# A fused attention and mixture-of-experts layer: the constant under the roots on GpSimd, the scatter in five steps, and new step lists

## The reference

```python
# 1: flow attention, 16 heads of 16, then a feed-forward block
q, k, v = sigmoid(x@Wq+bq), sigmoid(x@Wk+bk), x@Wv+bv
sink_in = n / sum((q+eps) * (cumsum(k)+eps));  src_out = n / sum((k+eps) * (cumsum(q)+eps))
cons_sink = sum((q+eps) * (cumsum(k*src_out)+eps)) / n
cons_src  = exp(clip(sum((k+eps) * (cumsum(q*sink_in)+eps)) / n, -1, 1))
a = q*sink_in/n @ cumsum(k (x) v*cons_src/cumsum(cons_src)*n) * sigmoid(cons_sink)
h = layernorm(x + a@Wo+bo)*g1+b1;  h = layernorm(h + gelu(h@W1+c1)@W2+c2)*g2+b2
x = layernorm(x + h)
# 2: eight experts of width 1024, each token goes to the one with the largest logit
e = argmax(x@router.T);  x = layernorm(x + square(relu(x@fc[e]))@proj[e].T)
```

## Time and profile before

| | |
|---|---|
| median of 3 runs | 828.53 us |
| lowest, highest | 828.28, 829.38 us |
| span of the profiled execution | 827.1 us |
| PE busy | 781.0 us (94%) |
| VectorE (DVE) busy | 579.8 us (70%) |
| GpSimd (POOL) busy | 337.6 us (41%) |
| ScalarE (ACT) busy | 309.9 us (37%) |
| chain that ended last | PE 88%, DVE 5%, issue 2%, ACT 2%, POOL 1% |

### The profile page before, as it was taken

How to read it: one execution, slowest core, us unless ns; L and a number is a source line. 1 busy time by engine, 2 the same in 40 slices (tenths; PEclk the granted TensorE clock), 3 DMA queues, 4 the chain that set the end, 5 groups by cost and what they waited for, 6 DMA issues and landing times.

```text
span 827.1 us, 18739 instructions
## 1 busy us (share of the span) xinstructions
PE 781.0 (94%) x6828; PEld 599.1 (72%) x6828; DVE 579.8 (70%) x1339; ACT 309.9 (37%) x571; POOL 337.6 (41%) x433
## 2 busy tenths in 40 slices
PE   7988899999999999999999989989999999999994
PEld 3466677677687687677777777778998787777762
DVE  7988878898988889889898884783654433433432
ACT  2333323523523633533543433342123444334442
POOL 8211513423642741750661663463324333234434
PEclk9999999999999999999999999999999999999998
DMA  7999995100100100100000032683769897878850
GB/s 252 279 330 329 325 323 174 52 1 2 52 28 1 53 27 2 52 27 2 27 27 2 27 112 107 204 282 100 252 209 380 341 337 294 329 293 299 296 203 13
DMA packets 75194, 133.22 MB, mean 161 GB/s; under 512 B 5726, under 2 KB 54112, under 8 KB 75105
## 3 DMA queue, kind: packets, MB, share of 16 engines
q1 hardware_dynamic: 71936, 123.57, 44.4%
q0 software_dynamic: 3168, 8.46, 2.8%
HBM read 89.35 MB, written 42.93 MB: 160 GB/s over the span
## 4 chain that ended last, share of the span: by engine, by line
PE 88%; DVE 5%; issue 2%; ACT 2%; POOL 1%; DMA 0%; POOLq 0%; ACTq 0%; SPq 0%; DVEq 0%
PE bank L950 11%; PE bank L985 11%; PE bank L837 7%; PE bank L849 7%; PE bank L869 6%; PE bank L880 6%; PE bank L649 6%; PE bank L799 5%; PE bank L815 4%; PE bank L765 4%; PE bank L997 4%; PE bank L965 4%; PE bank L658 2%; PE bank L687 2%; PE bank L679 2%
## 5 line engine op out<-in xcount | busy, mean ns | idle before, releaser
L1300 POOL TENSOR_TENSOR rstd<-vare,minus_half 128x1 f32<-128x1 f32 x96 | 59.2, 618 | 255.0 <-DVE vare L1575 254.5
L950 PE MATMUL bank<-xsT,fc 128*128 128x128 f32 x800 | 95.8, 279 | 0.7 <-issue 0.7
L950 PEld LDWEIGHTS bank<-xsT,fc 128*128 128x128 f32 x800 | 93.4, 195 | 3.7 <-issue 3.4
L1566 DVE TENSOR_TENSOR sm<-bank,upto 128x512 f32<-128x512 f32 x128 | 79.4, 682 | 19.1 <-PE bank L765 19.1
L985 PE MATMUL bank<-pj,act 128*128 x336 | 76.1, 380 | 0.5 <-issue 0.5
L1161 ACT ACTIVATE relu<-bank 128x512 f32<-128x512 f32 x68 | 40.1, 595 | 86.9 <-PE bank L950 59.0
L837 PE MATMUL bank<-n1T,w1s 128*128 128x256 f32 x256 | 67.5, 386 | 2.9 <-ACT hT L1110 2.4
L869 PE MATMUL bank<-n1T,w1s 128*128 128x256 f32 x256 | 67.4, 386 | 1.3 <-ACT hT L1127 0.8
L985 PEld LDWEIGHTS bank<-pj,act 128*128 128x128 f32 x336 | 62.3, 190 | 8.2 <-issue 0.7
L1355 POOL TENSOR_TENSOR mrstd<-mvare,minus_half 128x1 f32<-128x1 f32 x34 | 19.3, 566 | 118.8 <-DVE mvare L1784 118.8
L880 PE MATMUL bank<-w2s,hT 128*128 128x256 f32 x256 | 66.3, 387 | 0.3 <-ACT hT L1127 0.3
(11 more groups left out here) (267 smaller groups left out, 1644.4 us busy)
## 6 DMA issues: line engine op xcount, KB each, us to landing
routed_rows<-empty SPq DMA_DIRECT2D x64, 520.0 KB, 8.3
fc<-in_fc SPq DMA_DIRECT2D x31, 1024.0 KB, 6.7
up_unit<-in_fc SPq DMA_DIRECT2D x24, 1024.0 KB, 8.3
pj<-in_pj SPq DMA_DIRECT2D x8, 1024.0 KB, 12.3
xrow<-in_fc SPq DMA_DIRECT2D x6, 1024.0 KB, 6.9
...
```

The costliest lines, as they stand in the source:

```text
L950: last = nc.tensor.matmul(h_bank[n][:, chunk(f)], fc[:, at, k, chunk(4 * n + f)], xsT[:, k, :], start=(k == 0), stop=(k == KT - 1))
L1300: nc.gpsimd.tensor_tensor(rstd[:, n, c], vare[:, n, c], minus_half[:], ALU.pow)\
L1566: nc.vector.tensor_tensor(sm[:, n], BANK4[n][:].rearrange("p (h t) -> p h t", h=4), upto[:].unsqueeze(1).broadcast_to([P, 4, P]), ALU.mult ...
```

## The change

Three things change in code, and all the step lists.

1. The addition of 1e-5 moves from VectorE to GpSimd, where it stands directly ahead of the power, as `(x + 1e-5) * 1.0`. `c_sum2`'s next VectorE instruction now waits for bn_aggr itself.
2. `d_count` on GpSimd is cut into five: `d_ids` (the ids) and four steps `d_count` 0 to 3 with one indirect DMA each.
3. `turn_k` (p_kt) gets waits, since it now stands ahead of `p_pairs`.

```diff
@@ turn_k, PE
                 if c == 0:
+                    ev["kp"].wait(pe, g, KT)
+                    if g == 0:
+                        pe.wait_ge(masks_done, ALL_MASKS)
+                        ev["v"].wait(pe, 1, 4)
@@ rsqrt, GpSimd
+                ev[f"ba{n + 1}"].wait(pool, g, c + 1)
+                nc.gpsimd.tensor_scalar(vare[:, n, c], mv[:, n, c, 1:2], EPS_LN, 1.0, ALU.add, ALU.mult)\
+                    .then_inc(S[f"ve{n + 1}"], 1)
                 ev[f"ve{n + 1}"].wait(pool, g, c + 1)
@@ scatter, GpSimd
-            def scatter(g, half, _):
+            def next_ids(g, half, _):
                 wait_scattered(pool, g, half)
                 ...
                 nc.gpsimd.tensor_scalar(mine, mine, L, None, ALU.add).then_inc(ids_next, 1)
+            def scatter(g, half, c):
+                if c == 0:
+                    pool.wait_ge(ids_next, g + 1)
+                    ... (the rows, the emptied tiles, the slots)
-                for c in range(NC):
-                    nc.gpsimd.indirect_dma_start(...)
+                nc.gpsimd.indirect_dma_start(...)
@@ store (routed tiles), GpSimd
+                M["aggr"].wait(pool, j, 1)
+                nc.gpsimd.tensor_scalar(mvare[:, j % 3], mmv[:, j % 3, 1:2], EPS_LN, 1.0, ALU.add, ALU.mult)\
+                    .then_inc(M["vare"].sem, 1)
@@ stats, finish, VectorE
-                nc.vector.tensor_scalar(vare[:, n, c], mv[:, n, c, 1:2], EPS_LN, None, ALU.add)...
-                nc.vector.tensor_scalar(mvare[:, s], mmv[:, s, 1:2], EPS_LN, None, ALU.add)...
```

The lists, in the parts that the prediction speaks of (each line is one engine's order; `x n` is the step's index):

```diff
@@ DVE_FIRST (group 0 unless told)
-a_proj 0..3, a_prod, a_proj 4, 5, a_dots1, t_head, a_share1, a_scan2 0, 1, t_xb, a_proj(1) 4, a_dots2,
+a_proj 0, t_head, a_proj 1..3, a_prod, a_proj 4, 5, a_dots1, t_xb, a_share1, a_scan2 0, 1, a_proj(1) 4, t_half1 0, a_dots2,
@@ PE_ORDER
-p_share2, d_count, a_proj 0, b_turn 0, a_proj 1 2 3, b_turn 1, a_proj 4, b_up 0, a_proj 5, p_kt 0, b_down 0, b_up 1,
-p_pairs 0, b_up 2, b_down 1, b_down 2, b_up 3, p_mix 0, a_dots1, p_out 0, b_down 3, b_up 4, c_route 0, p_pairs 1, p_kt 1,
-b_up 5, b_down 4, p_mix 1, p_out 1, b_up 6, a_share1, b_down 5, b_up 7, b_down 6, c_route 1, h_turn 0, p_pairs 2, h_turn 1,
-b_down 7, h_up 0, p_kt 2, h_up 1, h_down 0, ..., p_mix 2, a_dots2, p_out 2, ..., p_mix 3, a_comp, p_out 3, h_up 6, ...
+p_share2, d_count, b_turn 0, a_proj 0 1, b_turn 1, a_proj 2 3 4, b_up 0, a_proj 5, p_kt 0, b_up 1, b_down 0, b_up 2,
+p_pairs 0, b_down 1, b_up 3, b_down 2, p_mix 0, a_dots1, b_up 4, p_out 0, b_down 3, p_pairs 1, c_route 0, b_down 4, p_kt 1,
+b_up 5, p_mix 1, b_down 5, p_out 1, b_up 6, a_share1, b_up 7, c_route 1, b_down 6, h_turn 0, b_down 7, h_turn 1, p_kt 2,
+h_up 0, p_pairs 2, h_up 1, h_down 0, ..., p_mix 2, a_dots2, p_out 2, ..., p_mix 3, a_comp, h_up 6, c_route 3, p_out 3, ...
@@ DVE_ORDER
-..., c_sum2 0, 1, a_proj 0..5, a_prod, p_mask 0..3, c_sum3 0, 1, p_state 0, a_dots1, p_sums 0, p_mask 4..7, b_half, c_sum2 2,
-p_state 1, p_sums 1, a_share1, a_scan2 0, 1, p_mask 8..11, c_sum3 2, c_sum2 3, p_state 2, a_dots2, p_sums 2, ...
+..., c_sum2 0, a_proj 0..5, a_prod, p_mask 0..3, c_sum2 1, c_sum3 0, p_state 0, a_dots1, p_sums 0, c_sum3 1, p_mask 4..7,
+c_sum2 2, p_state 1, c_sum3 2, p_sums 1, c_sum2 3, a_share1, b_half, a_scan2 0, p_mask 8..11, a_scan2 1, c_sum3 3, a_dots2, ...
@@ ACT_ORDER
-p_share2, b_turn 0, a_proj 0 1 2, b_turn 1, a_proj 3, b_up 0, ...
+b_turn 0, a_proj 0 1, b_turn 1, a_proj 2 3, p_share2, b_up 0, ...
@@ POOL_ORDER
-p_xb, p_split, d_count, c_sum2 0, 1, c_sum3 0, 1, p_mix 0, 1, c_sum2 2, c_sum3 2, p_norm 0, 1, c_sum2 3, b_turn, p_mix 2, ...
+d_ids, p_xb, p_split, d_count 0, c_sum2 0, d_count 1, c_sum2 1, d_count 2, c_sum3 0, p_mix 0, c_sum2 2, c_sum3 1, p_norm 0,
+p_mix 1, b_turn, d_count 3, c_sum3 2, c_sum2 3, p_norm 1, p_mix 2, c_sum3 3, ...
@@ the ..._LAST lists
 on GpSimd d_count 5, 6 and 7 are cut up among c_sum2, c_sum3 and m_store; the last, d_count(7) 3, stands behind m_store 4
 on VectorE d_units and d_placed of group 7 stand one tile (m_finish) later
```

More of the change, by code:

```diff
@@ L124 @@
[L124 to L127, removed]
+    ("p_out", 0, 1), ("a_share1", 1, 0), ("p_kt", 0, 2), ("h_turn", 0, 0), ("h_turn", 0, 1), ("p_pairs", 0, 2),
@@ L128 @@
+    ("h_up", 0, 0), ("h_down", 0, 0), ("h_up", 0, 1), ("p_mix", 0, 2), ("h_up", 0, 2), ("h_down", 0, 1),
+    ("h_up", 0, 3), ("p_out", 0, 2), ("a_dots2", 1, 0), ("h_up", 0, 4), ("h_down", 0, 2), ("p_kt", 0, 3),
+    ("p_pairs", 0, 3), ("h_up", 0, 5), ("h_down", 0, 3), ("p_mix", 0, 3), ("a_comp", 1, 0), ("p_out", 0, 3),
+    ("h_down", 0, 4), ("h_up", 0, 6), ("h_down", 0, 5), ("h_up", 0, 7), ("h_down", 0, 6), ("h_down", 0, 7),
 ]
 PE_ORDER = [
-    ("p_share2", 0), ("d_count", 0), ("a_proj", 0), ("b_turn", 0), ("a_proj", 1), ("a_proj", 2), ("a_proj", 3),
@@ L132 @@
[L132 to L140, removed]
+    ("p_share2", 0), ("d_count", 0), ("b_turn", 0), ("a_proj", 0), ("a_proj", 1), ("b_turn", 1), ("a_proj", 2),
+    ("a_proj", 3), ("a_proj", 4), ("b_up", 0), ("a_proj", 5), ("p_kt", 0), ("b_up", 1), ("b_down", 0), ("b_up", 2),
@@ new lines @@
+    ("p_pairs", 0), ("b_down", 1), ("b_up", 3), ("b_down", 2), ("p_mix", 0), ("a_dots1", 0), ("b_up", 4),
+    ("p_out", 0), ("b_down", 3), ("p_pairs", 1), ("c_route", 0), ("b_down", 4), ("p_kt", 1), ("b_up", 5),
+    ("p_mix", 1), ("b_down", 5), ("p_out", 1), ("b_up", 6), ("a_share1", 0), ("b_up", 7), ("c_route", 1),
+    ("b_down", 6), ("h_turn", 0), ("b_down", 7), ("h_turn", 1), ("p_kt", 2), ("h_up", 0), ("p_pairs", 2),
+    ("h_up", 1), ("h_down", 0), ("h_up", 2), ("h_down", 1), ("h_up", 3), ("h_down", 2), ("h_up", 4), ("p_mix", 2),
@@ L141 @@
+    ("a_dots2", 0), ("p_out", 2), ("c_route", 2), ("h_down", 3), ("p_pairs", 3), ("p_kt", 3), ("h_down", 4),
+    ("h_up", 5), ("p_mix", 3), ("a_comp", 0), ("h_up", 6), ("c_route", 3), ("p_out", 3), ("c_logit", 0),
+    ("h_down", 5), ("h_up", 7), ("c_back", 0), ("h_down", 6), ("h_down", 7),
 ]
 PE_LAST = [
-    ("b_turn", 7, 0), ("m_turn", 0, 0), ("b_turn", 7, 1), ("d_count", 5, 0), ("b_up", 7, 0), ("b_up", 7, 1),
-    ("b_down", 7, 0), ("b_up", 7, 2), ("b_down", 7, 1), ("b_up", 7, 3), ("b_down", 7, 2), ("c_route", 6, 0),
@@ L199 @@
+    ("h_turn", 0, 1), ("h_up", 0, 0), ("h_up", 0, 1), ("h_up", 0, 2), ("p_mix", 0, 2), ("h_up", 0, 3),
+    ("p_pairs", 0, 3), ("h_up", 0, 4), ("p_norm", 0, 2), ("a_dots2", 1, 0), ("p_mix", 0, 3), ("h_up", 0, 5),
+    ("h_up", 0, 6), ("p_norm", 0, 3), ("h_up", 0, 7),
 ]
 ACT_ORDER = [
[L202 to L203 removed]
@@ L204 @@
[L204 to L208 removed]
+    ("b_turn", 0), ("a_proj", 0), ("a_proj", 1), ("b_turn", 1), ("a_proj", 2), ("a_proj", 3), ("p_share2", 0),
```

146 lines of the change are left out of this document (73 added, 73 removed), and 5 rows, old and new, of tables (DVE_LAST, POOL_LAST).

## The result

The changed kernel took 821.41 us (median of four runs, 817.9 to 823.8) beside 828.95 of the kernel before (828.3 to 829.9): ratio 0.988, 95% interval 0.985 to 0.992. In a later session it took 818.8 beside 830.9 (0.986, 0.982 to 0.989). The nine runs together have a median of 820.5. Its profiled execution has a span of 819.8 us, 7.3 less than before. The forecast was 822.6, faster.

A forecast was written before the change was run, and what follows sets the result against it. PE was nearly always busy from 91 to 817 us, so only its idle time, and VectorE's chain in the first stage, could be won. Terms +2.3-0.5-3.5-1.8-2.7+0.3 = -5.9 gave 821.2, plus 1.4: 822.6 us, range 817.0 to 830.5.

The forecast's parts named there:

- 1, the start: First stage: VectorE's `t_xb`, moved ahead of `a_share1`, waits for the router's weights and delays the chain; +2.3 us, bounds 0 to 3.5.
- 2, the period of group 2: Period of group 2: PE's 2.2 us wait for the value tile at `p_pairs` shrinks; -0.5 us, bounds 0 to -1.0.
- the slower rival: Second scans: VectorE becomes late beside GpSimd's long operations, through the shared ports; 831.6 us, chance 0.16.
- 3, the full periods: Five steady periods: moved steps cover PE's small waits, 0.7 us gained in each; -3.5 us, bounds 0 and -5.3.
- 4, the last period: Last period: `b_turn` 0 moves ahead on ScalarE, so waits on `n1T` and `xat` shrink; -1.8 us, bounds 0 and -2.8.
- 5, the change-over: Change-over to the experts: scatters issued singly between roots remove PE's waits for routed row and expert tile; -2.7 us.
- the cut of the scatter adds no DMA: nothing: GpSimd's scatter: issuing the four transfers as separate steps was claimed to cost nothing.
- 6, the constant: Addition under the roots, moved to GpSimd: each root 0.3 us later, paid only by the very last tile; +0.3 us.
- the lists leave 0.5 us or more for both: Steady periods: ScalarE's n1 and xrow, behind a root 0.3 us later, were claimed to have 0.5 us or more cover.
- (a): Rival: VectorE becomes late at the second scans, delaying a_dots2 by 1.5 us in six periods; 831.6 us, chance 0.16.
- (b): Rival: gaps only move in steady periods, and last period and change-over gain half; -0.1 us, 828.4 us, chance 0.12.
- (c): Rival: the start costs nothing and all gaps close; -10.5 us, 818.0 us, chance 0.15.

## Why the prediction came out right, step by step

**1, the start: the mechanism right; the excess is mostly the clock of one run (+2.3, measured +6.2 in the profile shown).** The product's delay was 3.6 us, inside the 2.9 to 4.0 forecast. At 43.85 PE's first `p_share2` was 4.2 us late (39.64 before), but in two other profiles of the same steps it stood at 40.63 and 41.75; the profile shown had a granted clock of 0.79 at 34 to 42 us, all the others 1.00 up to 46. The stage itself ended at 97.56, 95.92 (the run again) and 94.17 (the kernel with the scatter block, whose first stage is instruction for instruction the changed one), and with the constants on VectorE at 97.13. With the old first lists the ends are 91.39, 91.50, 91.57, 93.06, 94.83 and 94.99. They compare only at like clocks. Where the mean granted clock up to 92 us was 0.96, the old lists ended at 91.5 and 91.6 and the changed ones at 94.2; where it was 0.93, at 94.8 and 95.0 against 95.9 and 97.6. So the step is worth 1 to 2.7 us, and the 2.3 lies in it. The stall with `t_xb` has 1.1 of that by either pair: 94.17 against 93.08 with the step put back, and 95.93 against 94.83 in the old lists. What the term lacked was the clock: the earlier trace rows gave 0.98 there, and I took a stage's clock as fixed. Of the medians none shows the step; runs spread too far.

**2, the period of group 2 (-0.5, measured -3.0): mis-sized.** That the later start made it short, which I tried with the old first lists, isn't so: it is short with either start. Three things came that the term didn't have (that these are the whole of it is read off the rows, not shown by a run). The wait on `n1T` at the head of this period, the largest of the three in the earlier trace rows, stood at 95.08 and goes with the same move of `b_turn` on ScalarE that I priced only for the last period. The timeline of the kernel before, and of the changed one:

```profile
95.08 0.41 PE L860 MATMUL bank<-ident,n 128*128 128x128 f32 x2 [2.19 <-ACT n1T L1121]
...
104.01 1.15 PE L765 MATMUL bank<-qm,kT 32*128 32x256 f32 x16 [2.24 <-DVE vpad L1479]
...
136.28 2.27 PE L799 MATMUL bank<-sm,vpad 128*32 128x128 f32 x29
```

```profile
99.63 0.41 PE L868 MATMUL bank<-ident,n 128*128 128x128 f32 x2 [0.57 <-ACT n1T L1129]
...
101.42 3.54 PE L662 MATMUL bank<-wqkv,xT 128*128 128x256 f32 x8 [1.38 <-DVE kT L1576]
```

The wait on `n1T` fell from 2.19 to 0.57. The value tile's 2.24 went too, and 0.9 on the query product, against a new 1.38 on the key product. And `p_mix` 2 took 2.27 us for 29 matmuls, at full clock, where the changed kernel has 1.12 for 32: a stretched group of matmuls that shows as busy and hides a wait. The masks that it waits for stood behind VectorE's second scans. The timelines of VectorE and GpSimd, before and changed:

```profile
124.98 7.66 DVE L1450 TENSOR_TENSOR_SCAN cc<-ones_t,cc 128x512 f32<-128x512 f32 x4
128.29 3.26 POOL L1294 TENSOR_TENSOR x<-x,be2s 128x1024 f32<-128x1024 f32 x1
```

```profile
128.91 2.37 POOL L1302 TENSOR_TENSOR x<-x,be2s 128x1024 f32<-128x1024 f32 x1
131.38 3.27 DVE L1467 TENSOR_TENSOR_SCAN cc<-ones_t,cc 128x512 f32<-128x512 f32 x2
```

The rule of the Trainium skill that I had weighed for the slower rival (page "SBUF — State Buffer", section "SBUF: two separate sides") pays out here on the gain's side: the last of the four scans took 3.31 us beside the wide addition, 1.2 where nothing stands beside one, and in the changed kernel the addition is over before the scans begin and the masks come after two of them. The trace doesn't bear out "in full" for every operation: beside the masked queries (1.6 to 2.2 us each, at 100.04 to 103.77) the changed kernel's scans took 1.21 and 1.65, though the profile's spans on GpSimd are rough. And the pair of the earlier trace rows is not where the 3 us come from: with the old first lists it took 4.63 beside the same addition, and the period was as short, 58.2. Nor is 3.0 a firm figure: the old period took 61.0, 61.1, 61.1, 62.7 and 62.7 us in five kernels with the same steps in it, the new one 58.0 to 58.2 in nine.

**3, the full periods (-3.5, measured -3.1): right.** 0.86, 0.70, 0.39, 0.71 and 0.40. The waits at `p_out` 1 and 3 are gone. The margin was nearly used up: 0.15 us of slack at `a_dots2`, not 0.7. With the constants back on VectorE the next thin place shows, the masks at `p_mix` 1, with 0.5 us.

**4, the last period (-1.8, measured -1.1): the size a little off.** The prediction took 2 of the 4.1 us on `n1T` for this period; it was 1.53, since the 2.2 in the earlier trace rows is group 2's. It fell to 0.56, and of the 1.4 us on `xat` 1.0 went; a new one of 0.5 us stands at `p_kt` (on `acc`), which now comes sooner.

**5, the change-over (-2.7, measured -6.4): right in sign, wrong in its reason.** I priced the removal of PE's waits at 555 with the cut as the cause. The cut alone costs 4.1 us in the old lists and, taken away, 7.2 in the new. What it does depends on what PE, VectorE and ScalarE have around it: the new order has `c_choose`, the squares and the expert tiles where their waits are covered. The old change-over also held more than the idle time that I priced: of the 6.4 us, 4.0 are idle time of PE over the whole part (6.1 to 2.0 us) and 2.3 are busy time, with a granted clock of 0.98 in the old one (0.96 in its first 46 us) and 1.00 in the new. The step that failed is "the cut of the scatter adds no DMA: nothing". It has a due time, the reuse of `xrow` two groups on.

**6, the constant (+0.3, measured +0.1 at the end): wrong as a whole.** The last tile's output multiply waits 0.97 us for its root, 0.69 before; but VectorE's own addition ahead of it is gone, and the tail as a whole is 0.1 us longer (192.3 in all ten profiles with the constant on GpSimd, 192.2 in the four without). The term had 0.3 us for the addition and 0.2 for the wait behind it; in this tile they are 0.19 and 0.09. In the steady periods it is free, as said. But "the lists leave 0.5 us or more for both" was argued, not read; in the old lists there is a stretch, the change-over, where it costs 3.8 us, and in the new lists it is worth some 3 us in the profile, which I put down to the relief of VectorE and had left at nothing.

**The rivals.** (a) did not come: a_dots2 isn't waited for. (b) did not come as a whole, but in part: in a steady period the waits on `xat` (0.3 us) and the query product (0.2) went and one of 0.3 on `n1T` came, so that 0.5 of the 1.06 us closed. (c)'s end, 818.0, is nearly as near to the nine runs' median of 820.5 as the forecast's 822.6 is, but its first half, a start that costs nothing, isn't in the profiles.

No version tried beats the changed kernel by more than the runs can tell. Left open: no run has the new lists without both the cut and the constant, or the periods' new lists with the old end. The runs with the old first lists show that the gain lies in the lists behind the first stage (58.2 us for the period of group 2, 317.7 for the five, 99.5 for the change-over); which moved step closed which wait there is read off the rows.
